# Shared-key attention: the causal mask of the scores' diagonal blocks is added by VectorE in PSUM instead of by TensorE products

## The chip, the cores and the metric

The program runs on one core of a Trainium2 chip. Its engines are TensorE (PE; its weight loads are shown as PEld), VectorE (DVE), ScalarE (ACT), GpSimd (POOL) and SyncE (SP, which issues DMAs). The metric is the device time of one execution in microseconds, lower is better.

## The reference

A decoder of four layers on x of 4 x 512 x 128, with twelve sub-blocks in a row, each followed by a residual and a layer norm. The change is in one of them, the attention of layer 2, in which keys and values share a projection and the keys are scaled. It has 16 heads of 64 values and a causal mask:

```
q = x @ w_q * (1.0 / jnp.sqrt(jnp.asarray(d, x.dtype)))
q = q.reshape(b, L, h, v).transpose(0, 2, 1, 3)
kv = (x @ w_kv).reshape(b, L, h, v).transpose(0, 2, 1, 3)
k = kv * (1.0 + k_weights)
logits = jnp.einsum('bhik,bhjk->bhij', q, k)
mask = jnp.tril(jnp.ones((L, L), dtype=bool))
logits = jnp.where(mask, logits, jnp.asarray(-1000000.0, logits.dtype))
a = jax.nn.softmax(logits, axis=-1)
y = jnp.einsum('bhij,bhjv->bhiv', a, kv)
y = y.transpose(0, 2, 1, 3).reshape(b, L, h * v)
return y @ w_o
```

## The kernel before

The sub-block is the function `shared_kv_attention`. Every engine runs a program of its own, written out by hand in program order, and the engines meet at semaphores; nothing reorders the program. The unit of work is a pair of heads `R` of one batch (8 pairs a batch, 32 in all): head `a` = 0 lies on partitions 0 to 63, head 1 on 64 to 127, so a product for both is a pair of matmuls on the two row halves of TensorE's array. A step of the outer loop has four turns `t`, one per tile of 128 queries or keys.

The scores are computed twice. First, three steps ahead of use (`LOOK`), `scores` (L2154) makes them with queries on partitions: for the tile `qt` of queries, all keys up to its own tile, 128 to 512 columns, into banks 0 and 1 or 2 and 3 by turns. Their diagonal block needs the causal mask, since the maximum over the keys is taken from them. L2158 adds it with four more bf16 products, `halves` times `tri`: an identity cut in two halves of 64 rows, times a triangle of -2^40. `maxima` (L2310, VectorE) then takes the negative maxima of both heads. GpSimd splits them into three bf16 parts once in two steps (`split`, L2262 to L2265), TensorE turns them (`turn_maxima`, L2166, at the end of odd steps), and ScalarE copies them to SBUF (L2390). Second, `scores_turned` (L2181) makes the scores with keys on partitions and adds the turned maxima (L2184). ScalarE takes the exponential (L2372), GpSimd zeroes what the causal mask excludes (L2270) and adds up (`add_up`), and `weigh` (L2196) multiplies by the values a step later. `sums` (L2207) gives the denominators, which ScalarE copies (L2354) and VectorE inverts (L2322, one tile a turn) and applies (L2328, once a step).

On TensorE a turn is: `scores` of step + 3, `scores_turned` of this step, `weigh` of the step before, and one projection of step + 4: `project_q` at t = 0 (L2127), `project_k` at t = 1 (L2133), `project_v` at t = 2 (L2140). Projections, turned maxima, sums and the output share one bank (`M_BANK`): `take` waits until the last reader of it is done, so L2140 waits for VectorE's read of the keys (`weigh_keys`, L2316). `scores` of turn i waits for the maxima of turn i - 2:

```python
                    if i >= 2:
...
                        pe.wait_ge(s["maxed"], i - 1)
```

On VectorE a turn is: `maxima`, then `invert`; after that the keys at t = 1, and `normalize` behind t = 3. Steps -3 to -1, the prologue, have only `scores` and projections; the last three steps have no `scores`. At the end of a batch, `project_out` (L2216, 32 matmuls), the residual (L1257) with its statistics (L1268, L1271), `rescale` (L1278) and `turn_x` (L1291) are put in.

`Chain` makes an instruction increment a semaphore of its own engine and has the engine wait for it, so that the next one reads what it wrote. `wb` takes a tile of the bf16 constants out of `bconst`, which one DMA loads at the start.

Of the kernel before, what the change touches and what calls it, by code (L numbers as in the profile page):

```python
# [11 lines left out]
ALU = mybir.AluOpType  # L12
AX = mybir.AxisListType

P = 128
# [8 lines left out]
MASKED = -float(2 ** 40)  # L24
# [30 lines left out]
def columns(groups):  # L55
    at, out = 0, {}
    for g, items in groups.items():
        for n, c in items:
            out[g, n] = (at, c)
            at += c  # L60
    return out, at
# [11 lines left out]
def places():  # L73
    at, out = 0, {}
    for groups in PLACES:
# [4 lines left out]
        for g, over in LATER.items():  # L80
# [7 lines left out]
S_AT = {g: columns({g: items}) for g, items in STREAMED.items()}  # L88
S_N = max(n for _, n in S_AT.values())
GROUPS = ["const"] + list(RESIDENT)  # L90
B_CONSTS = [("ident", P), ("halves", 2 * P), ("tri", 2 * P), ("sel", 2 * P), ("selhe", 4 * 8 * P),
            ("stacked", 32)]
B_AT, B_N = columns({"b": B_CONSTS})

# [27 lines left out]
def w(k, group, name, rows=P):  # L122
    at, n = R_AT[group, name]
    at += W_AT[group] - min(a for (g, _), (a, _) in R_AT.items() if g == group)
    return k.weights[0:rows, at:at + n]
# [8 lines left out]
def wb(k, name, rows=P):  # L134
    at, n = B_AT["b", name]
    return k.bconst[0:rows, at:at + n]
# [1118 lines left out]
def residual(k, dve, chain, s, b, y, read=None):  # L1255

    ins = dve.tensor_tensor(k.resid[:, :, :], y, k.xs[:, b], ALU.add)  # L1257
    if read:
        ins.then_inc(s[read], 1)
        dve.wait_ge(s[read], b + 1)  # L1260
    else:
        chain(ins)
    statistics(k, dve, chain, s)
# [11 lines left out]
def rescale(k, dve, s, b):  # L1275
    dve.wait_ge(s["rstd_ready"], b + 1)
    for t in range(NT):
        last = dve.tensor_scalar(k.xs[:, b, t, :], k.resid[:, t, :], k.mv[:, t, 0:1], k.rstd[:, t:t + 1],  # L1278
                                 ALU.subtract, ALU.mult)
    last.then_inc(s["x_ready"], 1)  # L1280
# [387 lines left out]
WD = 64  # L1668
# [405 lines left out]
def shared_kv_attention(k):  # L2074
    nc, ps = k.nc, k.ps
# [6 lines left out]
    S_BANK, T_BANK, Z_BANK, M_BANK = (0, 2), 4, 6, 7  # L2082
# [3 lines left out]
    def batch_at(step, at):  # L2086
        b, r = divmod(step - at, PAIRS)
        return b if r == 0 and 0 <= b < BATCH else None

    with ExitStack() as ctx:  # L2090
        def sb(n, shape, dt=F32):
            return ctx.enter_context(nc.sbuf_tensor(f"skv_{n}", shape, dt))

        kw1 = sb("kw1", [P, PAIRS])
        qT = sb("qT", [P, RING, SEQ])
        kT = sb("kT", [P, RING, SEQ])
# [6 lines left out]
        probs = sb("probs", [P, 2, 2, NT, SEQ])  # L2103
        total = sb("total", [P, 2, 2, SEQ])
        inv = sb("inv", [P, 2, SEQ])
        halves, tri, sel = (wb(k, n).rearrange("p (c n) -> p c n", c=2) for n in ("halves", "tri", "sel"))
        ones = w(k, "const", "one")
        wo = w(k, name, "wo").rearrange("p (r d) -> p r d", r=PAIRS)
        mt_ps = ps[:, M_BANK, :].bitcast(BF16)
# [1 line left out]
        with phase(k, "chain", "pool_chain", "cleared", "q_ready", "k_ready", "v_ready", "q_sb", "k_sb", "v_sb", "scores",  # L2111
# [3 lines left out]
            def _(pe):  # L2115
# [27 lines left out]
                def scores(R, qt):  # L2143
                    i, r = R * NT + qt, R % RING
                    if qt == 0:
                        pe.wait_ge(s["q_sb"], R + 1)
                        pe.wait_ge(s["k_sb"], R + 1)
                    if i >= 2:

                        pe.wait_ge(s["maxed"], i - 1)  # L2150
                    n = (qt + 1) * P
                    for a in range(2):
                        at, bank = slice(WD * a, WD * a + WD), S_BANK[i % 2] + a
                        pe.matmul(ps[:, bank, 0:n], qT[at, r, qt * P:n], kT[at, r, 0:n], start=True, stop=True)  # L2154
                    for a in range(2):
                        at, bank = slice(WD * a, WD * a + WD), S_BANK[i % 2] + a
                        for c in range(2):
                            last = pe.matmul(ps[:, bank, qt * P:n], halves[at, c, :], tri[at, c, :], start=False, stop=True,  # L2158
                                             skip_group_check=True)
                    last.then_inc(s["scores"], 1)  # L2160

                def turn_maxima(g):
# [135 lines left out]
            @block.vector  # L2298
            def _(dve):
                chain = Chain(dve, s["chain"])  # L2300
                chain(dve.tensor_scalar(kw1[:, :], w(k, name, "kw"), 1.0, None, ALU.add))

                def maxima(R, qt):
                    i, g = R * NT + qt, R // G
                    if qt == 0 and R % G == 0 and g >= 4:

                        dve.wait_ge(s["split"], g - 3)
                    dve.wait_ge(s["scores"], i + 1)
                    bank, at = S_BANK[i % 2], 2 * (R % G)
                    dve.tensor_reduce(negmax[:, g % 4, qt, at:at + 2], ps[:, bank:bank + 2, 0:(qt + 1) * P], AX.X,  # L2310
                                      ALU.max, negate=True).then_inc(s["maxed"], 1)

                def weigh_keys(R):
                    dve.wait_ge(s["k_ready"], R + 1)
                    r = R % PAIRS
                    dve.tensor_scalar(kT[:, R % RING, :], ps[:, M_BANK, :], kw1[:, r:r + 1], None, ALU.mult  # L2316
                                      ).then_inc(s["k_sb"], 1)

                def invert(R, t):
                    at = inv[:, R % 2, t * P:(t + 1) * P]  # L2320
                    dve.wait_ge(s["sum_sb"], R + 1)
                    dve.reciprocal(at, at).then_inc(s["inverted"], 1)  # L2322

                def normalize(R):
                    dve.wait_ge(s["inverted"], NT * (R + 1))
                    dve.wait_ge(s["z_out"], R + 1)
                    at = zT[:, R % OUT_RING, :]
                    dve.tensor_tensor(at, inv[:, R % 2, :], at, ALU.mult).then_inc(s["normalized"], 1)  # L2328

                for step in range(FIRST, LAST):  # L2330
                    if batch_at(step, ADD_AT) is not None:
                        b = batch_at(step, ADD_AT)
                        dve.wait_ge(s["y_ready"], b + 1)
                        residual(k, dve, chain, s, b, ps[:, M_BANK, :].rearrange("p (t d) -> p t d", t=NT), "y_read")
                    if batch_at(step, RESCALE_AT) is not None:
                        rescale(k, dve, s, batch_at(step, RESCALE_AT))
                    for t in range(NT):
                        if 0 <= step + LOOK < ALL:
                            maxima(step + LOOK, t)
                        if 3 <= step < ALL + 3:  # L2340
                            invert(step - 3, t)
                        if t == 1 and step + MAKE < ALL:
                            weigh_keys(step + MAKE)
                    if 3 <= step < ALL + 3:
                        normalize(step - 3)
# [635 lines left out]
def build(nc, xin, xTin, ctxT, m1q, m1k, m3q, m3k, wres, wstr0, wstr1, wstr3, bc, out):  # L2981
    k = Kernel()
    k.nc = nc
    with ExitStack() as ctx:
# [94 lines left out]
        arrive("L2a")  # L3079
        depart("L2f")  # L3080
        shared_kv_attention(k)
        cross_attention(k, "L2x", R8)
        arrive("L2f")
# [90 lines left out]
def bf16_consts():  # L3174
    out = np.zeros((P, B_N), np.float32)

    def put(n, m):
        at, c = B_AT["b", n]
        out[:m.shape[0], at:at + c] = m
    put("ident", np.eye(P))  # L3180
    q, kk = np.arange(P)[:, None], np.arange(P)[None, :]
    r = np.arange(P)[:, None] % 64
    both = lambda m: np.concatenate([np.concatenate([m[64 * c:64 * c + 64]] * 2) for c in range(2)], 1)
    put("halves", np.concatenate([np.arange(P)[None, :] == r + 64 * c for c in range(2)], 1))
    put("tri", both(np.where(kk > q, MASKED, 0.0)))

    put("sel", np.concatenate([np.broadcast_to(r // PARTS == c, (P, P)) for c in range(2)], 1))

    put("stacked", np.concatenate([np.eye(32)] * PARTS))

    she = np.zeros((64, 4, 8, P))
    for pair in range(4):
        for e in range(8):
            for a in range(2):
                she[(2 * pair + a) * 8 + e, pair, e, 64 * a:64 * a + 64] = 1.0
    put("selhe", she.reshape(64, -1))
    return out.astype(mybir.dt.np(BF16))
# [84 lines left out]
```

## Time and profile before

| | us |
|---|---|
| median of 3 runs | 3564.88 |
| lowest, highest | 3562.05, 3566.03 |
| the profiled execution | 3560.01 |
| its span | 3558.3 |

The span runs from the first to the last instruction of the profiled execution; the time of that execution has 1.7 us around it. Times in the rows are microseconds from the start of the span. A matmul row's own length is its latency and overlaps with the next; how long the engine is held by it is read from start to start. An fp32 product is recorded as two passes, each with a load of weights, so a pair of them is "x4"; a bf16 product is one. The sub-block of the change has its first matmul at 1980.28.

### The profile page before, as it was taken

The page shows a single profiled execution, that of the slowest core. Times are in us where ns is not written, and L with a number is a line of the kernel's source. Part 1 is how long each engine was busy: PE and PEld are TensorE (multiplying, and loading weights), DVE is VectorE, ACT ScalarE, POOL GpSimd, SP SyncE. Part 2 cuts the span into 40 slices and gives each one's busy share as a digit, 9 for nine tenths or more (in the row PEclk, how much of TensorE's full clock was granted, in tenths as well). Part 3 has the DMA queues.
Part 4 walks back from the last instruction along what each step waited for, and adds up shares of the span by engine and source line. Part 5 has one row for each costly group of instructions (what it writes and reads, how often), then busy time and mean ns, then how long its engine had stood idle before and what let it go on. Part 6 is the DMA issues. An engine that isn't in the chain of part 4 may idle for free. (4 is left out here: it accounts for less than half of the span.)

```text
span 3558.3 us, 41277 instructions
## 1 busy us (share of the span) xinstructions
PE 2880.4 (81%) x14768; PEld 1337.2 (38%) x14768; DVE 2106.9 (59%) x4175; ACT 1306.5 (37%) x2243; POOL 882.6 (25%) x1147
## 2 busy tenths in 40 slices
PE   4996879665555998879797899997785599699998
PEld 1332434221112443535354434434333233254555
DVE  5874841478777545555555355555667678464444
ACT  2664642333432552020211243332553266355221
POOL 2101100257546103030303254445215200110000
PEclk9997889888777999889899899999786699799999
DMA  5212200100001200000000000000300221220000
GB/s 136 42 28 59 47 19 1 47 0 0 0 0 31 60 12 1 1 1 0 1 1 1 17 1 1 1 1 1 61 12 0 34 42 34 73 51 8 1 1 12
DMA packets 39979, 74.60 MB, mean 21 GB/s; under 512 B 13048, under 2 KB 31916, under 8 KB 35936
## 3 DMA queue, kind: packets, MB, share of 16 engines
q1 hardware_dynamic: 39776, 71.96, 9.3%
q8 instruction: 119, 1.95, 0.2%
q14 instruction: 84, 0.69, 0.1%
HBM read 26.28 MB, written 1.05 MB: 8 GB/s over the span
## 5 line engine op out<-in xcount | busy, mean ns | idle before, releaser
L1630 POOL TENSOR_TENSOR mamba_dbu<-mamba_du,mamba_b 128x512 f32<-128x512 f32 x128 | 256.0, 2033 | 134.1 <-ACT mamba_b L1613 134.1
L1597 PE MATMUL ps<-mamba_hc,weights 128*128 128x512 f32 x256 | 167.1, 745 | 97.1 <-DVE mamba_hc L1655 96.7
L1644 DVE TENSOR_TENSOR_SCAN mamba_h<-mamba_da,mamba_dbu 128x512 f32<-128x512 f32 x128 | 211.3, 1653 | 18.3 <-ACT mamba_da L1618 18.3
L164 POOL TENSOR_SCALAR vareps<-mv 128x4 f32<-128x4 f32 x24 | 6.1, 254 | 760.6 <-DVE mv L1271 463.0
L534 DVE TENSOR_REDUCE L3a_negmax<-ps 128x1 f32<-128x512 f32 x256 | 162.5, 684 | 52.1 <-PE ps L294 51.6
L2310 DVE TENSOR_REDUCE skv_negmax<-ps 128x2 f32<-128x256 f32 (+3 forms) x128 | 105.1, 823 | 147.4 <-PE ps L2158 147.4
L534 DVE TENSOR_REDUCE L0a_negmax<-ps 128x1 f32<-128x512 f32 x256 | 162.5, 684 | 50.1 <-PE ps L294 49.6
L397 ACT ACTIVATE L0a_probs<-ps 128x512 f32<-128x512 f32 x256 | 143.7, 599 | 76.1 <-PE ps L313 74.5
L397 ACT ACTIVATE L3a_probs<-ps 128x512 f32<-128x512 f32 x256 | 143.7, 599 | 74.1 <-PE ps L313 72.5
L2372 ACT ACTIVATE skv_probs<-ps 128x1024 f32<-128x1024 f32 (+3 forms) x128 | 90.1, 704 | 205.3 <-PE ps L2184 205.3
L2045 PE MATMUL ps<-stream,moa_xm 128*128 128x128 f32 x1024 | 153.7, 296 | 1.4 <-DVE moa_xm L2067 1.4
L2067 DVE TENSOR_TENSOR moa_xm<-moa_zT,ps 128x512 f32<-128x512 f32 x128 | 87.7, 688 | 105.8 <-PE ps L2036 105.8
L2045 PEld LDWEIGHTS ps<-stream,moa_xm 128*128 128x128 f32 x1024 | 129.7, 199 | 33.0 <-issue 28.0
L294 PE MATMUL ps<-stream,L3a_qs 128*128 128x512 bf16 x256 | 100.1, 394 | 30.1 <-DMA stream<-stream 17.9
L2897 ACT ACTIVATE rffn_sg<-ps 128x512 f32<-128x512 f32 (+1 forms) x96 | 57.0, 596 | 180.4 <-PE ps L2853 180.3
L2941 DVE TENSOR_TENSOR rffn_hid<-rffn_sg,ps 128x512 f32<-128x512 f32 (+1 forms) x96 | 65.2, 685 | 97.4 <-ACT rffn_sg L2897 72.8
L2322 DVE RECIPROCAL skv_inv<-skv_inv 128x128 f32<-128x128 f32 x128 | 118.4, 936 | 7.7 <-ACT skv_inv L2354 7.7
L294 PE MATMUL ps<-stream,L0a_qs 128*128 128x512 bf16 x256 | 100.3, 395 | 26.2 <-DMA stream<-stream 12.5
L1597 PEld LDWEIGHTS ps<-mamba_hc,weights 128*128 128x128 f32 x256 | 45.4, 215 | 193.5 <-DVE mamba_hc L1655 191.7
L178 ACT COPY xT<-ps 128x512 f32<-128x512 f32 x8 | 4.7, 586 | 295.9 <-PE ps L172 295.9
L1953 PE MATMUL ps<-stream,xT 128*128 128x512 f32 x256 | 110.5, 592 | 0.0
L2852 PE MATMUL ps<-xT,stream 128*128 128x512 f32 (+1 forms) x192 | 100.7, 606 | 11.5 <-DVE rffn_hid L2941 11.5
(624 smaller groups left out, 6776.8 us busy)
## 6 DMA issues: line engine op xcount, KB each, us to landing
stream<-stream SPq DMA_DIRECT2D x32, 192.0 KB
stream<-gate_up_down_in SPq DMA_DIRECT2D x1, 4352.0 KB, 14.0
stream<-value_output_in SPq DMA_DIRECT2D x1, 4096.0 KB, 12.0
stream<-ffn_in SPq DMA_DIRECT2D x1, 2888.0 KB, 9.5
L0a_qs<-L0a_qs SPq DMA_DIRECT2D x16, 128.0 KB
L0x_qs<-L0x_qs SPq DMA_DIRECT2D x16, 128.0 KB
L1x_qs<-L1x_qs SPq DMA_DIRECT2D x16, 128.0 KB
L2x_qs<-L2x_qs SPq DMA_DIRECT2D x16, 128.0 KB
```

The lines of the kernel that those rows point to most:

```text
L294: pe.matmul(ps[:, i % S_RING, :], qs[:, n % HALVES, h, a * P:(a + 1) * P], ks[:, n % HALVES, h, :], start=True, stop=True).then_inc(s["sco ...
L397: act.activation(probs[:, J % PB, a, :], ps[:, T_BANK + i % T_RING, :], ACT.Exp, scale=scale).then_inc(s["exped"], 1)
L534: dve.tensor_reduce(negmax[:, hh // G % 4, a, hh % G:hh % G + 1], ps[:, i % S_RING, :], AX.X, ALU.max, negate=True).then_inc(s["maxed"], 1)
L1597: pe.matmul(ps[:, 4 + j, :], k.ident, hc[:, (J * n + j) % RING, :], start=n == 0, stop=n == N - 1).then_inc(s["summed"], 1)
L1630: pool.tensor_tensor(dbu[:, i % RING, :], du[:, j, :], bsb[:, n % AHEAD, :], ALU.mult).then_inc(s["dbu_ready"], 1)
L1644: dve.tensor_tensor_scan(out=hs[:, i % RING, :], data0=da[:, i % RING, :], data1=dbu[:, i % RING, :], initial=0.0, op0=ALU.mult, op1=ALU.a ...
L1953: pe.matmul(ps[:, 4 + i % 4, :], k.xT[:, t * P:(t + 1) * P], value[:, e, :], start=True, stop=True).then_inc(s["values"], 1)
L2045: last = pe.matmul(ps[:, 4 + t, 0:D], xm[:, i % RING, t * P:(t + 1) * P], output[:, i % E, i // E, :], start=i == 0, stop=i == PAIRS * E - 1)
L2310: dve.tensor_reduce(negmax[:, g % 4, qt, at:at + 2], ps[:, bank:bank + 2, 0:(qt + 1) * P], AX.X, ALU.max, negate=True).then_inc(s["maxed"], 1)
L2322: dve.reciprocal(at, at).then_inc(s["inverted"], 1)
L2372: act.activation(probs[:, step % 2, :, t, t * P:], ps[:, T_BANK:T_BANK + 2, t * P:], ACT.Exp, scale=scale).then_inc(s["exped"], 1)
L2852: pe.matmul(ps[0:nr, bk, :], gate[:, e % EXPERTS3, a0:a0 + nr], x, start=True, stop=True)
```

## The change

The four products L2158 of each turn are taken out. In `maxima`, VectorE first adds a causal triangle to the diagonal block of both heads, reading and writing it in PSUM, and waits for itself; then it takes the maxima as before. The triangle is a new bf16 constant of 128 x 128 with -2^40 above the diagonal, read for both heads through a broadcast. The mask has the same value as before. The constants `halves` and `tri` stay, since another sub-block uses them.

```diff
-B_CONSTS = [("ident", P), ("halves", 2 * P), ("tri", 2 * P), ("sel", 2 * P), ("selhe", 4 * 8 * P),
+B_CONSTS = [("ident", P), ("halves", 2 * P), ("tri", 2 * P), ("causal", P), ("sel", 2 * P), ("selhe", 4 * 8 * P),
             ("stacked", 32)]
...
-        halves, tri, sel = (wb(k, n).rearrange("p (c n) -> p c n", c=2) for n in ("halves", "tri", "sel"))
+        sel = wb(k, "sel").rearrange("p (c n) -> p c n", c=2)
+        causal = wb(k, "causal").unsqueeze(1).to_broadcast([P, 2, P])
...
                     for a in range(2):
                         at, bank = slice(WD * a, WD * a + WD), S_BANK[i % 2] + a
-                        pe.matmul(ps[:, bank, 0:n], qT[at, r, qt * P:n], kT[at, r, 0:n], start=True, stop=True)
-                    for a in range(2):
-                        at, bank = slice(WD * a, WD * a + WD), S_BANK[i % 2] + a
-                        for c in range(2):
-                            last = pe.matmul(ps[:, bank, qt * P:n], halves[at, c, :], tri[at, c, :], start=False, stop=True,
-                                             skip_group_check=True)
+                        last = pe.matmul(ps[:, bank, 0:n], qT[at, r, qt * P:n], kT[at, r, 0:n], start=True, stop=True)
                     last.then_inc(s["scores"], 1)
...
                     dve.wait_ge(s["scores"], i + 1)
                     bank, at = S_BANK[i % 2], 2 * (R % G)
+                    diag = ps[:, bank:bank + 2, qt * P:(qt + 1) * P]
+                    chain(dve.tensor_tensor(diag, diag, causal, ALU.add))
                     dve.tensor_reduce(negmax[:, g % 4, qt, at:at + 2], ps[:, bank:bank + 2, 0:(qt + 1) * P], AX.X,
                                       ALU.max, negate=True).then_inc(s["maxed"], 1)
...
+    put("causal", np.where(kk > q, MASKED, 0.0))
```

On TensorE, the end of turn t = 2 and turn t = 3 of a steady step (`project_v`, then `scores`, `scores_turned`, `weigh`, `sums`) stand in this order before:

```order
L2140 MATMUL ps<-weights,xT 128x512
L2154 MATMUL ps<-skv_kT,skv_qT 128x512 x2
L2158 MATMUL ps<-bconst 128x128 x4
L2181 MATMUL ps<-skv_qT,skv_kT 128x128 x2
L2184 MATMUL ps<-skv_mt,bconst 128x128 x2
L2196 MATMUL ps<-skv_probs,stream 64x128 x2
L2207 MATMUL ps<-skv_total,weights 64x512 x2
```

And in the changed kernel, whose lines have other numbers (L2155 is `scores`, L2177 `scores_turned`):

```order
L2141 MATMUL ps<-weights,xT 128x512
L2155 MATMUL ps<-skv_kT,skv_qT 128x512 x2
L2177 MATMUL ps<-skv_qT,skv_kT 128x128 x2
L2180 MATMUL ps<-skv_mt,bconst 128x128 x2
L2192 MATMUL ps<-skv_probs,stream 64x128 x2
L2203 MATMUL ps<-skv_total,weights 64x512 x2
```

The fp32 pair of `scores_turned` now follows the fp32 pair of `scores` with nothing between them; the rest is in the order it had.

On VectorE, the turns t = 1 and t = 2 of a steady step with their waits (stage_9 counts the scores, stage_0 is the engine's own chain, stage_21 the copied sums, stage_4 the keys' product), before:

```order
L2310 TENSOR_REDUCE skv_negmax<-ps 128x2 [waits stage_9]
L2322 RECIPROCAL skv_inv<-skv_inv 128x128 [waits stage_21]
L2316 TENSOR_SCALAR skv_kT<-ps,skv_kw 128x512 [waits stage_4]
L2310 TENSOR_REDUCE skv_negmax<-ps 128x2 [waits stage_9]
L2322 RECIPROCAL skv_inv<-skv_inv 128x128 [waits stage_21]
```

And in the changed kernel (L2307 is the new addition, L2308 the maxima, L2320 the inversion, L2314 the keys):

```order
L2307 TENSOR_TENSOR ps<-ps,bconst 128x2x128 [waits stage_9]
L2308 TENSOR_REDUCE skv_negmax<-ps 128x2 [waits stage_0]
L2320 RECIPROCAL skv_inv<-skv_inv 128x128 [waits stage_21]
L2314 TENSOR_SCALAR skv_kT<-ps,skv_kw 128x512 [waits stage_4]
L2307 TENSOR_TENSOR ps<-ps,bconst 128x2x128 [waits stage_9]
L2308 TENSOR_REDUCE skv_negmax<-ps 128x2 [waits stage_0]
L2320 RECIPROCAL skv_inv<-skv_inv 128x128 [waits stage_21]
```

The addition takes over the wait for the scores, and the maxima wait for the addition; the keys stand behind one more instruction.

## Rows read from the trace of the kernel before

**Rows 1.** The page, part 1: busy us, share of the span, instructions of each engine.

```profile
PE 2880.4 (81%) x14768; PEld 1337.2 (38%) x14768; DVE 2106.9 (59%) x4175; ACT 1306.5 (37%) x2243; POOL 882.6 (25%) x1147
```

**Rows 2.** Busy time by engine, TensorE's granted clock, DMA, in the steady stretch.

```profile
core 0: us, PE busy (x) PEld busy (x) DVE busy (x) ACT busy (x) POOL busy (x), PEclk, DMA share, GB/s
2020.00:2420.00 400.00, 384.92 (x2464) 162.44 (x2460) 221.70 (x292) 150.12 (x234) 197.34 (x393) 1.00 0.00 1
```

**Rows 3.** Waits, 2020 to 2420: total us, times, longest.

```profile
DVE skv_negmax L2310 <- PE ps L2158: 132.0, 99, 4.0
...
PE ps L2166 <- ACT skv_inv L2354: 10.1, 13, 0.8
...
PEld ps L2181 <- ACT skv_mt L2390: 4.6, 14, 0.5
```

**Rows 4.** Groups by line and form, 2020 to 2420.

```profile
L2158 PE MATMUL ps<-bconst 64*128 64x128 bf16 x448 | 31.2, 216 | 0.0
```

**Rows 5.** Timeline of TensorE, one turn (t = 3): start us, length us.

```profile
2217.89 1.13 PE L2140 MATMUL ps<-weights,xT 128*128 128x512 f32 x2
...
2219.91 0.28 PE L2158 MATMUL ps<-bconst 64*128 64x128 bf16 x4
...
2220.02 0.44 PE L2181 MATMUL ps<-skv_qT,skv_kT 64*128 64x128 f32 x4
...
2220.72 1.03 PE L2207 MATMUL ps<-skv_total,weights 128*64 128x512 f32 x4
```

**Rows 6.** The same turn in narrow stretches: the second passes of fp32 pairs.

```profile
2219.48 0.60 PE L2154 MATMUL ps<-skv_kT,skv_qT 64*128 64x512 f32 x2
...
2220.18 0.28 PE L2181 MATMUL ps<-skv_qT,skv_kT 64*128 64x128 f32 x2
...
2220.61 0.28 PE L2196 MATMUL ps<-skv_probs,stream 128*64 128x128 f32 x2
...
2221.15 0.60 PE L2207 MATMUL ps<-skv_total,weights 128*64 128x512 f32 x2
```

**Rows 7.** The same turn: loads of weights (PEld).

```profile
2219.96 0.30 PEld L2181 LDWEIGHTS ps<-skv_qT,skv_kT 64*128 64x128 f32 x4
...
2220.61 0.25 PEld L2207 LDWEIGHTS ps<-skv_total,weights 128*64 128x64 f32 x4
```

**Rows 8.** Timeline of VectorE over one step, with the idle time ahead.

```profile
2213.15 0.69 DVE L2310 TENSOR_REDUCE skv_negmax<-ps 128x2 f32<-128x512 f32 x1 [2.52 <-PE ps L2158]
...
2215.86 0.75 DVE L2316 TENSOR_SCALAR skv_kT<-ps,skv_kw 128x512 f32<-128x512 f32 x1 [1.15 <-PE ps L2133]
...
2216.83 0.96 DVE L2310 TENSOR_REDUCE skv_negmax<-ps 128x2 f32<-128x768 f32 x1 [0.22 <-PE ps L2158]
...
2217.70 0.94 DVE L2322 RECIPROCAL skv_inv<-skv_inv 128x128 f32<-128x128 f32 x1
...
2220.23 1.23 DVE L2310 TENSOR_REDUCE skv_negmax<-ps 128x2 f32<-128x1024 f32 x1 [1.59 <-PE ps L2158]
...
2223.74 0.42 DVE L2310 TENSOR_REDUCE skv_negmax<-ps 128x2 f32<-128x256 f32 x1 [0.69 <-PE ps L2158]
```

**Rows 9.** VectorE reading PSUM: timeline at a batch's end, a group elsewhere.

```profile
2194.04 0.69 DVE L1257 TENSOR_TENSOR resid<-ps,x_tok 128x512 f32<-128x512 f32 x1 [6.84 <-PE ps L2216]
...
2194.77 0.87 DVE L1268 BATCH_NORM_STATS2 stats<-resid 128x6 f32<-128x128 f32 x4
...
L582 DVE TENSOR_TENSOR L0a_zn<-ps,L0a_inv 128x128 f32<-128x128 f32 x16 | 4.7, 292 | 0.6
```

**Rows 10.** Timeline in the prologue, VectorE and TensorE.

```profile
2000.04 0.69 DVE L2310 TENSOR_REDUCE skv_negmax<-ps 128x2 f32<-128x512 f32 x1 [0.63 <-PE ps L2158]
...
2001.08 0.75 DVE L2316 TENSOR_SCALAR skv_kT<-ps,skv_kw 128x512 f32<-128x512 f32 x1 [0.36 <-PE ps L2133]
...
2001.93 1.12 PE L2140 MATMUL ps<-weights,xT 128*128 128x512 f32 x2
```

**Rows 11.** DMA issues: KB each, us to landing.

```profile
bconst<-bconst_in SPq DMA_DIRECT2D x1, 1256.0 KB, 6.0
```

## The prediction

> **What bounds the kernel now.** I read the page first, then the stretch of the shared-key stage in a table of stretches, then the waits and the groups inside it, then one step of it instruction by instruction on TensorE and VectorE.
>
> The page says only that TensorE carries the whole program, at 81% [rows 1], in a mixture of a dozen stages. The change touches one of them, which runs from about 1,980 to 2,478 us. In its steady 400 us TensorE is busy for 384.9 us at a granted clock of 1.00, VectorE for 221.7, ScalarE and GpSimd for less than half of the time [rows 2]. VectorE waits 132 us for the very instructions that the change removes [rows 3]; TensorE's own waits in the table are short, the largest being 10.1 us at `turn_maxima` for the copy of the sums. So TensorE's order of instructions sets the pace: an instruction taken out of it shortens the stage, and one given to VectorE costs nothing as long as it fits into VectorE's idle time.
>
> **What the removed products take on TensorE.** The group of L2158 has 448 instructions of 216 ns, and a union of 31.2 us in the 400 [rows 4]. Neither number is what they hold the engine for. 216 ns is the latency of one, and the union overlaps its neighbours. The right number is from start to start. The last turn (t = 3) of one step shows it. L2158 starts at 2219.91, the next line, L2181, at 2220.02 [rows 5]: four matmuls cost 0.11 us, since the two row halves run side by side.
>
> But the products also stand between two fp32 groups, and there is a second cost behind them. An fp32 pair comes in two passes. Narrow stretches of the timeline show the second passes [rows 6]: that of L2154 at 2219.48, that of L2181 at 2220.18, so 0.70 us from the one to the other. What is work in it? 512 columns of the pass of L2154 and 128 of the first pass of L2181. The rows price both where nothing intervenes: the second pass of L2196 (128 columns) starts at 2220.61, L2207 follows at 2220.72, so 0.11; L2207's second pass (512 columns) follows at 2221.15, so 0.43 [rows 5, 6]. Together 0.54. The other 0.16 us (0.165, I take, at the rows' resolution) is the masks' 0.11 and 0.055 of waiting for weights: the fp32 weights of L2181 start to load at 2219.96, only when the second mask pass starts [rows 7], because the masks' own weights occupied the place before them. With the masks gone this load can run behind the second pass of L2154, as L2207's does behind L2196: it starts at 2220.61 with that pass, and costs nothing [rows 6, 7].
>
> A rule of the Trainium skill speaks against this last point: page "TensorE: Matmul & The Clock Gate", section "The mechanism", says that a weight load overlaps with running matmuls only when it goes to another group of rows. L2207's load goes to the same rows as L2196 and is hidden all the same, so this trace disagrees with it; what the rule would give is the first rival.
>
> How many turns gain this? `scores_turned` follows `scores` directly in 29 steps of 4 turns, 116 in all. In 15 of them (t = 0 of the even steps) L2181 waits for ScalarE's copy of the turned maxima instead; the table has 14 such waits, 4.6 us together [rows 3]. That chain starts at `turn_maxima`, ahead of `scores`, and ends no sooner when `scores` gets shorter, so there the gain is nothing. Left are 101 turns x 0.165 = **16.7 us**.
>
> In the three steps of the prologue there is only `scores` and projections, 12 turns. There VectorE is late: in one step L2316 (the keys) starts at 2001.08 and lasts 0.75, and L2140 starts at 2001.93 when it is done [rows 10]. A further addition on VectorE takes back there about what the masks gave: between the end of the scores of one step's last turn and L2140, the chain of the new instructions (t = 3, 0 and 1, then the keys) comes to about what it was. I count 3 of these turns at 0.1: 0.3 us.
>
> **What VectorE gets.** One TENSOR_TENSOR of 128x256 per turn, fp32, from PSUM to PSUM with a bf16 tile of SBUF as the second input. No row writes to PSUM from VectorE. The nearest read PSUM and write SBUF: 128x128 takes 292 ns and 128x512 takes 0.69 us [rows 9], a line that gives 0.425 us for 256. Where the next instruction waits for the one before, as the new maximum does (L1257 at 2194.04, then its statistics at 2194.77), it starts 0.04 after its end [rows 9]; so 0.47 us per turn, bounded below by the 0.29 of the smaller form and above by the 0.73 of the larger one with its wait. In the steady stretch 112 turns x 0.47 = 52.6 us fall on VectorE, 221.7 + 52.6 = 274 of some 385: 71%.
>
> Does it fit at each place? The steady step has VectorE idle before nearly every maximum: 2.52 us at t = 1, 0.22 at t = 2, 1.59 at t = 3, 0.69 at t = 0, and 1.15 before the keys [rows 8]. With 0.47 more in each turn the keys still start when their product is ready; t = 2, which follows them at once, ends 0.47 later less the 0.11 that its scores come earlier, into the 1.59; t = 3 likewise, into the 0.69, of which 0.1 to 0.2 is left after the turn has become shorter. Who waits for VectorE? `scores` for the maximum two turns back, some 6.5 us; POOL's `split` once in two steps, whose result TensorE takes a step later; L2140 for the keys, which are done at 2216.61 while L2140 starts at 2217.89 [rows 5, 8], 1.28 us to spare. None comes to hold TensorE. So this part costs nothing in the steady steps. If that cover were gone, each turn would cost its 0.47.
>
> **Small parts.** `bconst` grows by 32 KB; its 1256 KB land in 6.0 us [rows 11], so at most 0.15 us at the start. 1,024 records fewer on TensorE's side: nothing. The last three steps have no `scores`; they start earlier by the whole gain and keep their waits.
>
> **Sum.** 16.7 + 0.3 - 0.1 = about 17 us. The profiled execution took 3560.0 us (span 3558.3), so 3543 for it; the median of the runs is 3564.9, 4.9 us higher, and on that footing the changed kernel takes **3548 us**.
>
> **The rivals.**
> First, *the weights are not hidden* (0.13). If the fp32 load of L2181 can't run behind the second pass of L2154 on the same rows, it costs its length where the masks' small loads stood. The size is in the rows: with the masks in front, 0.055 of it was exposed after the 0.05 of one mask pass, so a whole load is about 0.105, and a turn gains 0.165 - 0.105 = 0.06: 101 x 0.06 = 6 us, 3559. For it: L2181's load starts late today. Against it: L2158's and L2207's loads run behind passes on their own rows. This is also what the skill's rule makes of it.
>
> Second, *the addition in place is slow and VectorE becomes the bound* (0.05); it ends on the other side. VectorE has 178 us idle in the 400. Two waits of 6.84 us for `project_out` [rows 9] cannot be filled, and 16 go with the shorter stretch: (178 - 14 - 16) / 112 = 1.3 us a turn. From 1.3 us per addition VectorE sets the pace. At 1.6 us, more than twice the price of the larger form, it needs 221.7 + 179 + 14 = 415 us for what takes 400 now: 15 us slower, 3580. For it: no row writes PSUM from VectorE, reading and writing the same addresses. Against: even the maximum over 128x1024 takes only 1.23 us [rows 8].
>
> Third, *TensorE's clock* (0.05). The granted clock is 1.00 through the steady stretch [rows 2], also across the 0.7 us that TensorE waits in each step. With fewer matmuls it could fall to the lower of its two levels now and then. At half clock each microsecond costs half; 34 us of it would eat the gain, so this gives about 3565, give or take 7. The same page's section "What's actually happening" has the clock depend on how busy the engine has recently been; no row here shows it falling at 96% busy.
>
> Fourth, *more than counted* (0.04): if the prologue and the waiting turns gained too, 128 x 0.165 = 21 us, 3543 or somewhat less.
>
> **Numbers.** The forecast has 0.73, with a range of its own of 3543 to 3553 (a gain of 12 to 22 us, which covers a gain of 0.11 alone in all turns, 14 us less, and the full 0.165 in all). To hold 8 in 10 the whole range takes in the first rival and the spread of runs, 3562 to 3566, on the base: **3540 to 3559**. A change of 0.2%, 7.1 us, is about what this measurement tells from none. Faster by more: 0.73 + 0.04 + a little of the first and third = 0.80. Within it: most of the first and half of the third, 0.13. Slower: the second and the rest of the third, 0.07.
>
> **What would show it.** In the changed profile: from the second pass of the scores to the second pass of the turned scores at t = 3, 0.54 us instead of 0.70; the load of the turned scores' weights starting with the scores' second pass; TENSOR_TENSOR ps<-ps,bconst near 425 ns; VectorE near 71% busy in the steady stretch and its wait for the scores down by some 50 us; no row in which TensorE waits for the maxima or the keys outside the prologue; the waits at `turn_maxima` unchanged, those at L2181 for the copied maxima longer by 0.1 to 0.2 each; granted clock 1.00. I am wrong if L2154 is followed only after 0.1 us and more (first rival), if the addition takes over 1.3 us (second), or if the keys turn up as what L2140 waits for.

## The result and the profile after

| | us |
|---|---|
| before, 6 runs on the same chip | median 3565.23 (3559.43 to 3568.38) |
| changed, 6 runs | median 3548.16 (3547.28 to 3557.37) |
| ratio | 0.9960, 95% interval 0.9947 to 0.9973 |
| profiled execution of the changed kernel | 3557.37, span 3555.7 |

The change makes the kernel 0.4% faster, 17.1 us by the medians. Forecast were 3548 us and 17 us. The interval allows a gain of 9.6 to 18.9 us, so that the medians meet the forecast to 0.1 us is luck; the stage's own lengths below are the firmer test. The profiled execution happens to be the slowest of the six: its stage begins 10.7 us later than that of before, in stages that the change does not touch (shown below by a second profile), so the two profiles are compared inside the stage and not by their spans.

The stretch of [rows 2] and VectorE's wait and group in it, of the changed kernel:

```profile
2020.00:2420.00 400.00, 382.31 (x2102) 159.72 (x2102) 279.76 (x419) 156.81 (x245) 202.27 (x404) 1.00 0.00 1
```

```profile
DVE ps L2307 <- PE ps L2155: 79.2, 60, 3.4
...
PEld ps L2155 <- DVE skv_negmax L2308: 24.9, 33, 0.8
...
PE ps L2162 <- ACT skv_inv L2352: 10.1, 13, 0.8
...
PEld ps L2177 <- ACT skv_mt L2388: 6.8, 15, 0.6
```

```profile
L2307 DVE TENSOR_TENSOR ps<-ps,bconst 128x256 f32<-128x256 f32 x117 | 50.3, 430 | 82.3 <-PE ps L2155 79.2
```

VectorE is now busy for 70% of the stretch instead of 55%, and its wait for the scores fell from 132.0 [rows 3] to 79.2 us. The new addition takes 430 ns. TensorE is as busy as before and at the same clock; its wait at the turned maxima (L2162) is the same 10.1 us. The row of L2155's weight loads, which name VectorE's maxima as what they came after, is new, and the forecast had said that no such row would appear outside the prologue. It costs nothing: the load of L2155 at 2221.17 has 0.76 us of idle time before it, named after the maxima, and the load of L2154 at 2218.94 in the kernel before has the same 0.76 us, named "issue"; TensorE's matmuls have no idle time at either place. What it does in its time is another question, and the turn at t = 3 answers it. Narrow stretches of TensorE's timeline, first the second pass of the scores, then that of the turned scores:

```profile
2221.71 0.59 PE L2155 MATMUL ps<-skv_kT,skv_qT 64*128 64x512 f32 x2
```

```profile
2222.24 0.28 PE L2177 MATMUL ps<-skv_qT,skv_kT 64*128 64x128 f32 x2
```

and the load of the turned scores' first weights:

```profile
2221.71 0.19 PEld L2177 LDWEIGHTS ps<-skv_qT,skv_kT 64*128 64x128 f32 x2 [0.23 <-issue]
```

From second pass to second pass it is 0.53 us, where [rows 6] had 0.70. The load begins at 2221.71, together with the second pass of the scores on the same rows of the array, where in [rows 7] it began only with the second pass of the masks.

The stage as a whole is read from the first start of the scores to the last start of the turned scores. The two lines' groups, before and then after (the last two times are the first and the last start):

```profile
L2154 PE MATMUL ps<-skv_kT,skv_qT x512: 272/482/816, 1988.0 to 2421.3; 64*128 64x128 f32 x43, 64*128 64x384 f32 x43, 64*128 64x512 f32 x43, 64*128 64x256 f32 x42
L2181 PE MATMUL ps<-skv_qT,skv_kT x512: 272/481/693, 2011.7 to 2456.5; 64*128 64x512 f32 x43, 64*128 64x256 f32 x43, 64*128 64x128 f32 x43, 64*128 64x384 f32 x42
```

```profile
L2155 PE MATMUL ps<-skv_kT,skv_qT x512: 269/482/1006, 1998.7 to 2415.3; 64*128 64x128 f32 x43, 64*128 64x384 f32 x43, 64*128 64x512 f32 x43, 64*128 64x256 f32 x42
L2177 PE MATMUL ps<-skv_qT,skv_kT x512: 269/481/694, 2022.3 to 2450.4; 64*128 64x512 f32 x43, 64*128 64x256 f32 x43, 64*128 64x128 f32 x43, 64*128 64x384 f32 x42
```

2456.5 - 1988.0 = 468.5 us before, 2450.4 - 1998.7 = 451.7 after: 16.8 us less. Of it the prologue (first scores to first turned scores) has 23.7 - 23.6 = 0.1, and the rest (first to last turned scores) 444.8 - 428.1 = 16.7, which is what the forecast had from 101 turns x 0.165. Turn by turn, from one second pass of the turned scores to the next, the two traces say it a little differently: 100 turns are shorter by 0.167 each, and 15 are as long as before. 14 of these are the waiting turns that were counted (the fifteenth of them opens the stretch). The other is t = 0 of the second step, where L2177 waits for ScalarE's exponential:

```profile
2031.40 1.13 PE L2177 MATMUL ps<-skv_qT,skv_kT 64*128 64x512 f32 x4 [0.20 <-ACT skv_probs L2370]
```

### The profile page after: what moved, and what is told of

Its sections match the earlier page's. It is cut to its first block and busy times, and to the rows that moved or that the text cites. A ratio compares the mean times of both kernels' runs of the same rounds, so it can differ in the third digit from the quotient of the medians.

```text
span 3555.7 us, 40334 instructions
## 1 busy us (share of the span) xinstructions
PE 2864.5 (81%) x14209; PEld 1331.3 (37%) x14256; DVE 2162.1 (61%) x4303; ACT 1305.5 (37%) x2243; POOL 883.7 (25%) x1147
## 3 DMA queue, kind: packets, MB, share of 16 engines
HBM read 26.31 MB, written 1.05 MB: 8 GB/s over the span
## 5 line engine op out<-in xcount | busy, mean ns | idle before, releaser
L2320 DVE RECIPROCAL skv_inv<-skv_inv 128x128 f32<-128x128 f32 x128 | 118.3, 936 | 7.9 <-ACT skv_inv L2352 7.9
L294 PE MATMUL ps<-stream,L3a_qs 128*128 128x512 bf16 x244 | 95.4, 393 | 31.6 <-DMA stream<-stream 18.3
L294 PE MATMUL ps<-stream,L0a_qs 128*128 128x512 bf16 x244 | 95.9, 396 | 27.2 <-DMA stream<-stream 12.5
L2307 DVE TENSOR_TENSOR ps<-ps,bconst 128x256 f32<-128x256 f32 x128 | 55.1, 430 | 89.6 <-PE ps L2155 86.4
L2850 PE MATMUL ps<-xT,stream 128*128 128x512 f32 (+1 forms) x192 | 100.3, 604 | 11.5 <-DVE rffn_hid L2939 11.5
```

The source lines that it names most:

```text
L294: pe.matmul(ps[:, i % S_RING, :], qs[:, n % HALVES, h, a * P:(a + 1) * P], ks[:, n % HALVES, h, :], start=True, stop=True).then_inc(s["sco ...
L2850: pe.matmul(ps[0:nr, bk, :], gate[:, e % EXPERTS3, a0:a0 + nr], x, start=True, stop=True)
```

## The experiments

The first four ran beside runs of the kernel before with a median of 3562.39 us, the last four beside runs with 3564.16; each ratio is to the runs beside it. The table has the medians, the ratios, and three lengths from the profiles, made as above: the whole stage, its prologue, and the rest.

| kernel | median us | ratio (95%) | stage | prologue | rest |
|---|---|---|---|---|---|
| before | | | 468.5 | 23.7 | 444.8 |
| changed | 3548.16 | 0.9960 (0.9947 to 0.9973) | 451.7 | 23.6 | 428.1 |
| `e1_no_mask` | 3547.47 | 0.9961 (0.9948 to 0.9973) | 450.8 | 22.6 | 428.2 |
| `e2_both_masks` | 3563.11 | 1.0005 (0.9996 to 1.0014) | 469.3 | 24.5 | 444.8 |
| `e3_half_products` | 3556.80 | 0.9987 (0.9979 to 0.9996) | 462.4 | 23.1 | 439.3 |
| `e4_three_adds` | 3554.20 | 0.9974 (0.9963 to 0.9986) | 459.3 | 30.7 | 428.6 |
| `e5_four_adds` | 3601.78 | 1.0109 (1.0095 to 1.0123) | 508.2 | 34.9 | 473.3 |
| `e6_moa_too` | 3561.82 | 0.9994 (0.9985 to 1.0003) | | | |
| `e7_no_mask_moa` | 3544.45 | 0.9947 (0.9934 to 0.9961) | | | |
| `e8_changed_again` | 3546.88 | 0.9955 (0.9942 to 0.9967) | 451.7 | 23.6 | 428.1 |

**TensorE's side alone.** The changed kernel without its addition:

```diff
-                    diag = ps[:, bank:bank + 2, qt * P:(qt + 1) * P]
-                    chain(dve.tensor_tensor(diag, diag, causal, ALU.add))
```

> Leaves the mask of the scores with queries on partitions out altogether: no TensorE products, no VectorE addition (the maxima then also see the keys that the mask excludes; the exponentials are zeroed there as before). It gives TensorE's side of the change alone. Theory A (the forecast's): VectorE's addition costs nothing in the 29 steady steps, so those gain what the changed kernel gains, 0 in the 15 turns that wait for the copied maxima and 0.167 us in the other 101, 16.9 us from the first turned scores to the last; only the prologue is better than in the changed kernel, by 1 to 1.5 us, since its turns t = 1 no longer wait 0.5 us each for the maxima. Time some 18 us under the kernel before. Rival: the addition costs something in every turn, through PSUM or through waits; then this kernel gains clearly more than 0.167 per turn, 20 us or more in all.

Measured: the rest of the stage takes 428.2 us against 428.1 in the changed kernel, so the addition costs nothing there. The prologue is 1.0 us shorter. The rival is out. By time the kernel is 14.9 us under the one before, where 18 were expected; the interval allows 9.6 to 18.5, so the times alone would not decide it.

**VectorE's side alone.** The changed kernel with the four products of L2158 put back behind the scores:

```diff
-                        last = pe.matmul(ps[:, bank, 0:n], qT[at, r, qt * P:n], kT[at, r, 0:n], start=True, stop=True)
+                        pe.matmul(ps[:, bank, 0:n], qT[at, r, qt * P:n], kT[at, r, 0:n], start=True, stop=True)
+                    for a in range(2):
+                        at, bank = slice(WD * a, WD * a + WD), S_BANK[i % 2] + a
+                        for c in range(2):
+                            last = pe.matmul(ps[:, bank, qt * P:n], halves[at, c, :], tri[at, c, :], start=False, stop=True,
+                                             skip_group_check=True)
```

> Keeps the four TensorE products and makes VectorE's addition as well (the mask is added twice, the maxima are the same). It gives VectorE's side alone. Theory A: between the first and the last turned scores nothing changes against the kernel before (within 0.3 us over 29 steps), though VectorE is busy for some 50 us more; the prologue gets 1 to 2 us longer, at the turns t = 1 that wait for the maxima two turns back. Total 1 to 2 us over before, not to be told from it by time. Rival: VectorE's writes into PSUM disturb TensorE's; then each turn gets longer, by 0.05 us or more, over 5 us in all.

Measured: 444.8 us for the rest, as before. The same stretch of the table of stretches, before and then with both, shows where the work went; VectorE has 15.6 us more to do in 120, TensorE is busy for the same 115.41:

```profile
2060.00:2180.00 120.00, 115.41 (x720) 45.65 (x718) 69.50 (x87) 47.28 (x74) 60.42 (x120) 1.00 0.00 1
```

```profile
2060.00:2180.00 120.00, 115.41 (x720) 45.55 (x716) 85.05 (x121) 47.80 (x75) 60.15 (x120) 1.00 0.00 1
```

The prologue got 0.8 us longer, a little under the 1 to 2 expected. Writing PSUM from VectorE beside TensorE's work disturbs nothing that can be measured.

**How the 0.167 us of a turn is made up.** The kernel before with half of its products (the maxima of half of each tile's queries then also see excluded keys):

```diff
-                        for c in range(2):
+                        for c in range(1):
```

> The kernel before with only the first of the two mask products of each head (the mask of the last 64 queries of each tile is left out). Theory A says that the products cost 0.107 us by their columns and 0.06 by a weight load that starts one pass late, and that one pass left in front still keeps that load from being hidden: 0.108 us of cost is left per turn, so the gain is 0.06 per turn, 6 us over 101 turns. Rival (the cost is by product, all alike): half of 0.167, 0.084 per turn, 8.5 us. Second rival (a load is hidden as soon as one pass less stands ahead): 0.167 - 0.053, 0.114 per turn, 11.5 us. The spacing of the second passes at t = 3 tells them apart: 0.65, 0.62 or 0.59 us.

Measured: the rest is 5.5 us shorter, 0.055 in each of 100 turns, and not 8.5 or 11.5. Narrow stretches of a turn at t = 3 give the second pass of the scores and that of the turned scores:

```profile
2217.84 0.59 PE L2154 MATMUL ps<-skv_kT,skv_qT 64*128 64x512 f32 x2
```

```profile
2218.49 0.28 PE L2181 MATMUL ps<-skv_qT,skv_kT 64*128 64x128 f32 x2
```

They are 0.65 us apart, the first of the three spacings that were named beforehand. So one product of each head costs 0.11 us and the second 0.055 more. A mask pass is 0.05 from start to start (2219.91 to 2219.96 in [rows 5] and [rows 7]), and the other 0.055 is there once, with one small load in front of the fp32 load as with two.

**How much VectorE can take.** The changed kernel with the addition three times, and then four times, in each turn:

```diff
                     chain(dve.tensor_tensor(diag, diag, causal, ALU.add))
+                    chain(dve.tensor_tensor(diag, diag, causal, ALU.add))
+                    chain(dve.tensor_tensor(diag, diag, causal, ALU.add))
```

> The changed kernel with the addition made three times in each turn (the maxima are the same). Theory A: VectorE gets 1.4 us per turn where the forecast put the point at which it becomes the bound at 1.3, so VectorE sets the pace or nearly does: a steady step takes about 13.7 us instead of 13.05, the prologue 5 us more, the whole 3558 to 3568 us, the gain gone. TensorE then waits for the maxima two turns back or for the keys. Rival: the idle time of VectorE can't be used to the full, since it is bound to places in the turn; then TensorE waits already well before that, and the time is over 3570 us.

> The changed kernel with the addition made four times in each turn (same maxima). With three, VectorE was busy for 114.9 of 120 us of the steady stretch and TensorE kept its pace of 13.3 us a step. Theory A: the fourth adds 0.47 us to each of 112 turns and nothing covers it; a steady step needs 12.8 + 1.9 = 14.7 us of VectorE, 1.3 us more than TensorE's pace, so the steady stretch gets 25 to 38 us longer than with three (the waits for the output projections can't be filled), and the prologue 2 to 3 us: 3580 to 3595 us, slower than the kernel before. Rival: VectorE still has idle time at the batch ends that it can use; then under 15 us more than with three, below 3570.

Measured, three: 428.6 us for the rest, 0.5 more than with one. A stretch of it, with VectorE at 96%:

```profile
2060.00:2180.00 120.00, 114.85 (x614) 44.84 (x614) 114.90 (x196) 48.70 (x78) 62.73 (x124) 1.00 0.00 1
```

Only the prologue paid, 7.1 us more than with one. TensorE waits there for the maxima two turns back and for the keys; in the timeline of TensorE:

```profile
2005.09 0.70 PE L2155 MATMUL ps<-skv_kT,skv_qT 64*128 64x256 f32 x4 [0.90 <-DVE skv_negmax L2310]
...
2009.48 1.69 PE L2141 MATMUL ps<-weights,xT 128*128 128x512 f32 x2 [1.74 <-DVE skv_kT L2316]
```

So the expectation that the gain would be gone was wrong, and so was its rival: 1.40 us a turn still fits. Four: 473.3, 44.7 us more than three, above the 25 to 38 expected, and slower than before by 1.1%. The same stretch:

```profile
2060.00:2180.00 120.00, 107.86 (x550) 41.14 (x546) 114.56 (x207) 43.52 (x68) 55.56 (x112) 0.96 0.00 1
```

VectorE is no busier than with three, TensorE holds its work back, and its mean clock in the stretch is 0.96 instead of 1.00. The limit lies between 1.40 and 1.87 us a turn. Since VectorE was full at 1.40, most of the fourth's 112 x 0.467 = 52 us had to come out as time, and 45 did.

**The same change where VectorE has no idle time.** The experts' attention of layer 1 (`wide_attend`) has the same products:

```diff
...
-                    pe.matmul(ps[:, bank, 0:n], qT[at, r, qt * P:n], kT[at, r, 0:n], start=True, stop=True)
-                for a in range(2):
-                    at, bank = slice(WD * a, WD * a + WD), S_BANK[i % 2] + a
-                    last = masked(ps[:, bank, qt * P:n], at, tri)
+                    last = pe.matmul(ps[:, bank, 0:n], qT[at, r, qt * P:n], kT[at, r, 0:n], start=True, stop=True)
...
+                diag = ps[:, b:b + 2, qt * P:(qt + 1) * P]
+                chain(dve.tensor_tensor(diag, diag, causal, ALU.add))
                 dve.tensor_reduce(negmax[:, qt, 2 * r:2 * r + 2], ps[:, b:b + 2, 0:(qt + 1) * P], AX.X,
```

> The same change made in the experts' attention of layer 1 as well, which has the same mask products in 64 turns (4 batches of 4 pairs of heads), but only 4 of every 16 turns have turned scores between them: in the other 12 VectorE and TensorE wait for each other in turn. Theory A (what decides is whether VectorE has idle time where it gets the addition): there it has not, a step of 4 such turns takes 4.17 us now with 3.0 us of maxima on VectorE, and with 1.87 more it needs 4.85; the way from the first scores to the first turned scores of a batch gets 1 to 2 us longer, 4 to 8 us for the four batches, and the time is 3552 to 3557 us, slower than the changed kernel. Rival (it pays off wherever it is made, 0.167 per turn): 64 x 0.167, 10 us faster than the changed kernel.

Measured: 3561.82 us, against 3546.88 for the changed kernel beside it, so 15 us are lost, more than the 4 to 8 expected. The table of stretches from the first scores to the first turned scores of the second batch, before and then here:

```profile
1531.87:1546.97 15.10, 13.14 (x109) 7.74 (x109) 9.45 (x12) 0.62 (x2) 1.81 (x5) 0.82 0.01 2
```

```profile
1540.08:1557.70 17.62, 14.36 (x57) 6.26 (x57) 14.03 (x24) 0.62 (x2) 1.80 (x5) 0.65 0.01 1
```

It is 2.5 us longer. Against the changed kernel of `e8_changed_again` the four batches' stretches are 2.6, 2.5, 2.6 and 2.0 us longer, where 1 to 2 were expected. TensorE's mean clock in them is 0.65 to 0.72, where it was 0.80 to 0.82. TensorE does less and waits more for VectorE: the timeline has waits like this one,

```profile
1714.33 1.71 PE L1709 MATMUL ps<-moa_kT,moa_qT 64*128 64x256 f32 x8 [1.18 <-DVE moa_negmax L1838]
```

where before the longest at that place was 0.93. These stretches account for 10 of the 15 us. Where the other 5 are stays open: between the two profiles, stretches of the program that the edit leaves alone differ as well, one by 4.0 us (from the third batch's last turned scores to the fourth's first scores, 123.7 us against 119.7).

**No mask in either attention.** No mask under the maxima in either attention; the edits are those of the first experiment and of the one above, without the addition:

> No mask under the maxima in either of the two attentions, neither products nor addition (the maxima are taken over the excluded keys of the diagonal block too; the exponentials are zeroed there as before). Theory A: in the experts' attention the chain between TensorE and VectorE loses two groups of products (0.16 each) per step of the start, so each batch gets about 1 us shorter, 4 us in all, on top of the 17 of the kernel without a mask in the shared-key attention alone: 3542 to 3545 us. Rival: the chain there is bound by VectorE's maxima alone; then nothing is gained, 3547.

Measured: 3544.45 us, 0.9947 of before; the interval (to 0.9961) overlaps that of the changed kernel beside it (from 0.9942), so by time alone the two are not apart. The same kind of stretch in the experts' attention is shorter:

```profile
1530.37:1543.95 13.58, 11.08 (x56) 5.50 (x56) 9.34 (x12) 0.61 (x2) 1.80 (x5) 0.80 0.01 2
```

13.58 against 15.10 us, and 1.5 in the third and fourth batch too, 2.0 in the first: more than the 1 us a batch that was expected, and against the rival, by which nothing would be gained. The price is another one: the row's maximum may come from an excluded key, and where that is far above all allowed keys the exponentials of the row get small. Whether that does harm with other inputs was not tried.

**The changed kernel again.**

> The changed kernel once more, beside the other three on the same chip. Its first profile had the shared-key stage begin 10.7 us later than in the profile of before, in stages that the change does not touch. Theory A: that is the spread of the clock in those stages, so this time the stage begins within 4 us of where it began before (1988 us) and the gain inside it, from the first scores to the last turned scores, is again 16.8 us within 0.2. Rival: something of the change (the longer bconst, other addresses) slows the stages ahead; then the beginning is again some 10 us late. Time 3545 to 3551.

Measured: the stage begins at 1988.3, 0.3 us after that of before, and takes 451.7 us again:

```profile
L2155 PE MATMUL ps<-skv_kT,skv_qT x512: 269/482/1006, 1988.3 to 2404.9; 64*128 64x128 f32 x43, 64*128 64x384 f32 x43, 64*128 64x512 f32 x43, 64*128 64x256 f32 x42
L2177 PE MATMUL ps<-skv_qT,skv_kT x512: 269/481/693, 2011.9 to 2440.0; 64*128 64x512 f32 x43, 64*128 64x256 f32 x43, 64*128 64x128 f32 x43, 64*128 64x384 f32 x42
```

The late beginning of the first profile was the spread of the stages ahead.

## Why the prediction was right

**What sets the pace.** That TensorE's order does, and VectorE's idle time is free, is shown from both sides: the products alone taken out give 16.6 us in the rest of the stage, the addition alone put in takes 0.0.

**0.165 us a turn.** Measured were 0.167 in each of the 100 turns that gain, 16.7 us in all. That the forecast's 101 x 0.165 is the same 16.7 is luck: the price was 0.002 too low and the count one turn too high. The split into 0.11 for columns and 0.055 for a late load was shown by the half-product kernel. The first rival, that the fp32 load can't be hidden behind a pass on the same rows, is refuted by the load's row above and by the 0.53 us from second pass to second pass. So the rule of the Trainium skill that a weight load overlaps only with matmuls on another group of rows (page "TensorE: Matmul & The Clock Gate", section "The mechanism") does not hold for this pattern. The same section names a load into the array's background weight buffer as a second case that overlaps; that is in line with this row, which can't show where the weights go.

**Turns that gain nothing.** The waiting turns gained nothing, as counted, and t = 0 of the second step, which waits for the exponential, gained nothing either and was not counted. The waits at the load grew from 4.6 us in 14 [rows 3] to 6.8 in 15.

**The prologue.** Forecast 0.3 us, measured 0.1. The chain named was the wrong one. I had L2140 waiting for the keys, because it starts 0.1 us after they end; but its row in [rows 10] has no idle time before it, so nothing held it there. In the changed kernel it is `scores` at t = 1 that waits, for the maxima of the turn before last. In the changed kernel's timeline:

```profile
2009.84 0.70 PE L2155 MATMUL ps<-skv_kT,skv_qT 64*128 64x256 f32 x4 [0.52 <-DVE skv_negmax L2308]
```

From the projection L2128 to this start it is 1.64 us in each of two steps, 1.18 in the kernel without a mask and 1.05 (from L2127) before; such a step takes 6.60 us, against 6.11 and 6.43. That took back most of what the first step of the prologue had gained. The kernel without a mask has the 1.0 us that could be had there.

**The addition.** 0.425 us forecast, 0.430 measured, 0.46 to 0.47 from start to start. The line through two sizes that write SBUF held for a write to PSUM.

**Where VectorE would become the bound.** The second rival's mechanism exists: four additions make the kernel slower than before. Its point was put at 1.3 us a turn and is above 1.40.

**The clock.** 1.00 in the steady stretch, as before; the third rival did not come. In `e5_four_adds` and `e6_moa_too`, where TensorE was made to wait, the clock fell, and in `e7_no_mask_moa`, which lacks the same products but has no addition to wait for, it was 0.80 at the same place. So that rival was tied to the second, not to the missing products.

**Small parts.** The 0.1 us for the longer `bconst` is too small for any of these runs to show.

## What to carry to other kernels

Price a small product by the distance between the starts of its neighbours with and without it, not by its own length: here four products with rows of 216 ns took 0.11 us together, plus 0.055 for the fp32 load that they kept from starting. Moving it to an idle engine pays in full when each turn's new work fits before the work that the busy engine waits for. Where the two engines answer each other turn by turn, as in the prologue and in the experts' attention, the same edit costs time.

## What the runs showed of the hardware

VectorE could be filled to 96% (114.9 of 120 us) with chained additions in place in PSUM while TensorE, writing other banks, kept the pace that it had with one addition a turn to within 0.5 us in 428. And where TensorE had to wait for VectorE, its granted clock was lower too (0.65 to 0.72 instead of 0.80 to 0.82 in the experts' attention). In the third batch there the matmuls of the kernel before run at full clock from 5.4 us after the first scores; in `e6_moa_too` TensorE first waits 1.18 us, they run at full clock at 6.9 us, and from 8.9 to about 16 us they have the lengths of the lower clock again. How much of the 2.5 us is the clock and how much the waits was not separated.
